# A gated attention and quantised layer on one core: the first key tile or the values move ahead of the output projection, and the opening is rewritten

## The reference

```python
x = x + tanh(g_xattn) * attention(layernorm(x), ctx, Wq, bq, Wk, bk, Wv, bv, Wo, bo)   # 16 heads of 32
x = x + tanh(g_ffn) * quantised(layernorm(x), weight_q, weight_scale, bias)

def quantised(x, weight_q, weight_scale, bias):
    x_scale = max(amax(|x|), 1e-6) / 127
    x_q = clip(round(x / x_scale), -128, 127)
    return (x_q @ weight_q.T) * x_scale * weight_scale + bias
```

## Time and profile before

| what | us |
|---|---|
| median of 3 runs | 916.76 |
| lowest and highest of these | 912.73, 916.80 |
| the profiled execution | 920.62 |
| its span, first to last instruction | 918.8 |
| PE busy | 836.2 (91% of the span) |
| DVE, ACT, POOL busy | 538.7, 513.4, 525.7 (56 to 59%) |
| first instruction of step 0 on PE | 76.07 after the span's start |

### The profile page before, as it was taken

The page is one execution under the profiler, slowest core; times in us unless marked ns, Lnnn a source line. Parts: engine busy times, 40 slices in busy tenths (PEclk is TensorE's granted clock), DMA queues, the critical chain, the costliest instruction groups (busy, mean ns, idle before and its releaser), DMA issues.

```text
span 918.8 us, 16063 instructions
## 1 busy us (share of the span) xinstructions
PE 836.2 (91%) x6304; PEld 522.9 (57%) x6304; DVE 538.7 (59%) x746; ACT 513.4 (56%) x708; POOL 525.7 (57%) x552
## 2 busy tenths in 40 slices
PE   4549989999999999999999999999999999999784
PEld 3336546656565666656565666656565666655451
DVE  2754365656655676656655676656655675654444
ACT  2323445656566665656566665656566665655633
POOL 0541344747475765747475755747475755745565
PEclk9777889999999999999999999999999999999997
DMA  8145031322314142312314142422314131111101
GB/s 269 43 143 164 26 120 46 119 69 64 122 41 144 47 147 65 126 61 68 121 47 138 47 145 68 119 74 60 122 42 144 35 116 46 35 49 44 59 24 68
DMA packets 39755, 80.15 MB, mean 87 GB/s; under 512 B 7168, under 2 KB 7808, under 8 KB 37632
## 3 DMA queue, kind: packets, MB, share of 16 engines
q1 hardware_dynamic: 38560, 77.97, 26.8%
q10 hardware_dynamic: 1120, 1.16, 0.4%
HBM read 62.30 MB, written 16.81 MB: 86 GB/s over the span
## 4 chain that ended last, share of the span: by engine, by line
PE 60%; DVE 13%; POOL 13%; issue 7%; DMA 3%; ACT 3%; SPq 0%; ACTq 0%; POOLq 0%; DVEq 0%
PE bank_a L298 22%; PE scores L331 6%; PE pv_ps L360 5%; PE bank_b L298 5%; PE scores L346 5%; PE sum_ps L362 5%; POOL x L1040 5%; DVE row_max L817 4%; PE bank_b L384 3%; POOL x L1053 3%; POOL o_lo L1044 3%; DVE q_unit L852 2%; PE bank_b L315 2%; DVE u_sb L862 1%; DVE q_amax L846 1%
## 5 line engine op out<-in xcount | busy, mean ns | idle before, releaser
L817 DVE TENSOR_REDUCE row_max<-scores 128x16 f32<-128x1920 f32 x64 | 138.2, 2159 | 158.5 <-PE scores L331 158.4
L1053 POOL TENSOR_TENSOR x<-x,u_sb 128x512 f32<-128x512 f32 x64 | 85.7, 1340 | 152.7 <-DVE u_sb L862 150.4
L604 ACT ACTIVATE probs<-scores 120x2048 f32<-120x2048 f32 x64 | 120.4, 1882 | 68.9 <-PE scores L350 68.9
L1044 POOL TENSOR_TENSOR o_lo<-on,o_hi 128x512 fp32r<-128x512 f32 x64 | 88.0, 1374 | 113.9 <-ACT o_hi L620 113.9
L807 DVE TENSOR_TENSOR xt_lo<-xt,xt_hi 128x512 fp32r<-128x512 f32 x64 | 69.6, 1108 | 96.6 <-ACT xt_hi L571 96.2
L1048 POOL TENSOR_TENSOR x<-x,gbias_r 128x512 f32<-128x512 f32 x64 | 82.3, 1287 | 51.9 <-ACT cen L626 51.6
L298 PE MATMUL bank_a<-xt_hi,wq_hi 128*128 128x512 f32 x248 | 106.1, 428 | 4.8 <-ACT v_sb L590 4.8
L1015 POOL TENSOR_TENSOR xt<-xt,rstd_b 128x512 f32<-128x512 f32 x64 | 100.2, 1591 | 16.6 <-DMA rstd_b<-rstd_rows 11.8
L331 PEld LDWEIGHTS scores<-k_sb,q_sb 32*128 32x128 f32 x2048 | 63.7, 188 | 64.7 <-issue 51.4
L298 PE MATMUL bank_a<-xt_lo,wq_hi 128*128 128x512 f32 x248 | 99.0, 399 | 0.0
L298 PE MATMUL bank_a<-xt_hi,wq_lo 128*128 128x512 f32 x248 | 98.9, 399 | 0.0
(11 more groups left out here) (155 smaller groups left out, 1663.4 us busy)
## 6 DMA issues: line engine op xcount, KB each, us to landing
xt<-in_x_t SPq DMA_DIRECT2D x16, 1024.0 KB, 5.5
x<-in_x SPq DMA_DIRECT2D x64, 256.0 KB, 3.0
out_x<-x SPq DMA_DIRECT2D x64, 256.0 KB, 2.1
x_in<-in_x SPq DMA_DIRECT2D x62, 256.0 KB, 3.8
rstd_b<-rstd_rows SPq DMA_DIRECT2D x16, 256.0 KB, 5.0
ctx_sb<-in_ctx_t SPq DMA_DIRECT2D x7, 360.0 KB, 5.0
probs<-in_wq SPq DMA_DIRECT2D x1, 1024.0 KB, 9.9
x<-in_wo SPq DMA_DIRECT2D x1, 1024.0 KB, 13.3
```

Source lines behind the costliest of these rows:

```text
L604: act.activation(probs[0:KEYS], scores[0:KEYS], ACT.Exp, scale=SCALE).then_inc(p_ready, 1)
L817: dve.tensor_reduce(row_max[:].rearrange("p (t r) j -> p r t j", r=ROWG)[:, :, :, j], scores[:, :, 0:QT * KEYS].rearrange("p r (t k) -> p ...
L1044: pool.tensor_tensor(o_lo[i % 2][:, j], on[:, j % 2], o_hi[i % 2][:, j].bitcast(F32), ALU.subtract).then_inc(o_split, 1)
L1053: pool.tensor_tensor(x1_of(m)[:, t], x1_of(m)[:, t], u_sb[:], ALU.add).then_inc(out_ready, 1)
```

## The change

**In every step.** In part 0 `project_k(pair, 0)` or `project_v(n - 1)` now comes right behind `scores_by_query(b, 0)`, in `bank_b`, and `project_o(m, 0)` behind it, in `bank_a`. `project_k(pair, 1)` follows in `bank_b` and waits for `k_ready` of the first key tile. In part 2 the same is done with `project_k(pair, 2)` or `project_v(n)` in `bank_a`, ahead of `project_o(m, 2)` in `bank_b`. ACT's `bias_k` or `copy_v` moves ahead of `high_o`. The banks of the neighbouring projections are exchanged to fit.

**In the front.** The inverse deviations of batches 0 and 1 no longer go through DRAM: PE spreads them over the partitions by four transposes into `sum_ps` (`spread_rstd`). For batch 0 DVE multiplies xt by it (`scale_x0`); for batch 1 ACT copies it to `rstd_b` and POOL multiplies as before. DVE alternates scaling xt, centring Wq and the rest of xt; POOL takes the rest of Wq. Wv is staged in `x1[1]` and loaded early, the tiles of batch 1 use `cen` as well, xt of batch 1 is loaded ahead of the five small constants. The splitting of Wo, the bias row (`fold_bias`, `fold_rows`) and the cast of the integer weights move into step 0, and POOL's four `bias_x` of batch 0 to the end of that step. The first `project_k` no longer waits for the bias of the keys.

```diff
             def load_x(n, t):
-                sp.wait_ge(x_stats, nth(n, QT, t) - 2 if n > 1 or t >= 2 else nth(0, QT, t))
-                load(x_landed[t % 2], x_in[:, t % 2], x_v[n, t])
+                if n == 1 and t >= 2:
+                    load(x1st_landed[t - 2], cen[:, t - 2, 0:D], x_v[n, t])
+                else:
+                    sp.wait_ge(x_stats, nth(0, QT, t) if n == 1 else nth(n, QT, t) - 2)
+                    load(x_landed[t % 2], x_in[:, t % 2], x_v[n, t])
...
+            def spread_rstd(n):
+                pe.wait_ge(x_pool, nth(n, 2, 1))
+                if n > 0:
+                    pe.wait_ge(x_scaled, nth(n - 1, DT, 3))
+                for t in range(QT):
+                    ins = pe.transpose(sum_ps[:, t * P:(t + 1) * P], ln_rstd[:, t:t + 1].broadcast_to([P, P]), ident_f[:])
+                ins.then_inc(rstd_spread, 1)
...
                 if is_batch(b):
                     scores_by_query(b, 0)
+                if i == 0:
+                    pe.wait_ge(v_ready, nth(1, 1))
+                if keys_next:
+                    project_k(pair, 0, bank_b)
+                if values_next:
+                    project_v(n - 1, bank_b)
                 if is_batch(m):
                     pe.wait_ge(o_split, nth(m, DT, 3))
-                    project_o(m, 0, bank_b)
+                    project_o(m, 0, bank_a)
                 if keys_next:
-                    project_k(pair, 0, bank_a)
-                    if is_batch(m):
-                        pe.wait_ge(x1_ready, nth(m, QT, 0))
+                    pe.wait_ge(k_ready, nth(pair, DT, 0))
                     project_k(pair, 1, bank_b)
-                if values_next:
-                    project_v(n - 1, bank_a)
...
+                if i == 0:
+                    fold_bias(bank_a)
...
-            project_q(0, 2, pv_ps)
+            project_q(0, 2, bank_a)
+            spread_rstd(1)
             pe.wait_ge(max_done, nth(0, DT, 0))
             scores_by_query(0, 1)
-            project_q(0, 3, bank_a)
+            project_q(0, 3, bank_b)
...
                 log_sums(i, 0)
                 invert_sums(i, 0)
+                if i == 0:
+                    act.wait_ge(wo_gated, 1)
+                    act.activation(flat(wo_hi), flat(wo_stage), ACT.Copy).then_inc(wo_hi_done, 1)
...
+                if keys_next:
+                    bias_k(pair, 0, bank_b)
+                if values_next:
+                    copy_v(n - 1, bank_b)
                 high_o(i, 0)
...
+            def scale_x0(c):
+                dve.wait_ge(rstd_spread, 1)
+                dve.wait_ge(xt_landed, 16)
+                dve.tensor_tensor(xt[:, c], xt[:, c], sum_ps[:], ALU.mult).then_inc(x_scaled, 1)
```

More of the change, by code:

```diff
@@ L237, in _ @@
             load(rest_landed, ident_b[:], consts_bf16)
-            load_xt(1)
-            for t in range(QT):
-                load_x(2, t)
+            load_x(2, 0)
+            load_x(2, 1)
             load_ctx(1)
+            load_x(2, 2)
+            load_x(2, 3)
             load_x(3, 0)
@@ L385, in quantised_layer, with fold_bias @@
                 ins.then_inc(ffn_done, 1)
+            def spread_rstd(n):
+                pe.wait_ge(x_pool, nth(n, 2, 1))
+                if n > 0:
+                    pe.wait_ge(x_scaled, nth(n - 1, DT, 3))
+                for t in range(QT):
+                    ins = pe.transpose(sum_ps[:, t * P:(t + 1) * P], ln_rstd[:, t:t + 1].broadcast_to([P, P]), ident_f[:])
+                ins.then_inc(rstd_spread, 1)
+            def fold_bias(bank):
+                pe.wait_ge(wo_gated, 1)
+                pe.wait_ge(bv_landed, 16)
+                for c in range(DT):
+                    ins = pe.matmul(bank[:], bv_c[:, c:c + 1].broadcast_to([P, P]), wo_stage[:, c],
+                                    start=c == 0, stop=c == DT - 1)
+                ins.then_inc(bv_ready, 1)
             def step(i):
@@ L501, in _ @@
             pe.wait_ge(consts_ready, 5)
-            pe.wait_ge(bk_landed, 16)
             pe.wait_ge(wk_landed, 16)
-            for j in range(DT):
-                project_k(0, j, scores[:, j])
+            project_k(0, 0, scores[:, 0])
+            project_k(0, 1, scores[:, 1])
+            pe.wait_ge(ident_landed, 16)
+            spread_rstd(0)
             pe.wait_ge(wq_landed, 16)
@@ L756, in _ @@
                 act.activation(wv_hi[:, c], wv_stage[:, c], ACT.Copy).then_inc(wv_hi_done, 1)
-            bias_q(0, 3, bank_a)
-            for c in range(DT):
-                high_x(1, c)
-            copy_v(0, bank_b)
+            bias_q(0, 1, bank_b)
+            bias_q(0, 2, bank_a)
+            act.wait_ge(rstd_spread, 2)
+            act.activation(rstd_b[:].rearrange("q (p t) -> q t p", t=QT), sum_ps[:].rearrange("q (t p) -> q t p", t=QT),
+                           ACT.Copy).then_inc(rstd_copied, 1)
+            bias_q(0, 3, bank_b)
+            high_x(1, 0)
+            copy_v(0, bank_a)
+            high_x(1, 1)
+            high_x(1, 2)
+            high_x(1, 3)
+            copy_v(1, bank_b)
             high_max(0)
-            copy_v(1, sum_ps)
-            copy_max(0, bank_a)
-            act.wait_ge(wv_lo_done, CT)
+            copy_max(0, pv_ps)
             for i in range(0, B):
@@ L942, in _ @@
             low_ctx(0)
-            dve.wait_ge(wq_mean, 1)
-            for c in range(DT):
-                dve.tensor_tensor(wq_stage[:, c], wq_stage[:, c], pv_ps[:], ALU.subtract).then_inc(wq_centred, 1)
-            for c in range(DT):
-                dve.wait_ge(wq_hi_done, c + 1)
-                dve.tensor_tensor(wq_lo[:, c], wq_stage[:, c], wq_hi[:, c].bitcast(F32), ALU.subtract).then_inc(wq_lo_done, 1)
+            scale_x0(0)
+            centre_wq(0)
+            scale_x0(1)
+            low_x(0, 0)
+            centre_wq(1)
+            scale_x0(2)
+            low_x(0, 1)
+            centre_wq(2)
+            scale_x0(3)
+            low_x(0, 2)
+            centre_wq(3)
+            low_x(0, 3)
+            for t in range(QT):
+                x_statistics(1, t)
+            maxima(0, 0)
+            x_statistics(2, 0)
+            x_statistics(2, 1)
+            maxima(0, 1)
+            low_x(1, 0)
+            low_x(1, 1)
+            maxima(0, 2)
+            low_x(1, 2)
+            low_x(1, 3)
+            maxima(0, 3)
+            low_max(0)
             dve.wait_ge(gates_ready, 1)
@@ L1094, in step @@
                 low_o(i, 3)
+                if i == 0:
+                    pool.wait_ge(bias_folded, 1)
+                    bias_x(i, 0)
+                    bias_x(i, 1)
                 bias_x(i, 2)
```

230 lines of the change are left out of this document (115 added, 115 removed).

## The result

| what | before | after |
|---|---|---|
| median of 4 runs each, us | 915.47 | 884.57 |
| lowest and highest | 912.73, 916.80 | 884.04, 886.75 |
| the profiled execution | 920.62 | 884.38 |
| its span | 918.8 | 882.6 |
| first instruction of step 0 on PE | 76.07 | 56.31 |

The ratio is 0.9671, with a 95% interval of 0.964 to 0.9701. The forecast was 883.2 us.

A forecast was written before the change was run, and what follows sets the result against it. PE bounds the loop; the front waits for data, DVE's gated Wo and a maximum. 920.62 - 19.6 (front) - 1.7 (step 0) - 12.3 (loop) = 887.0; the gain of 33.6 from 916.76 gives 883.2 us, range 876 to 896.5.

The forecast's parts named there:

- Step 0 starts at 56.5, gain 19.6: Front: step 0 begins at 56.5 us instead of 76.07, gain 19.6, bounds 53 and 61.
- First queries at 26.5, DVE the pace: Front: DVE's scalings, centrings and splits set the pace; PE ends the first query projection at 26.5 us, not 40.
- Clock in the front: Front: granted clock falls once near 23 us, PE idle between keys and queries, and once behind the 4.1 wait.
- Step 0, -1.7: Step 0: added bias product, key-bias waits and clock effects sum to -1.7 us, bounds -4 and +3.
- The -2.9: Step 0: the fold fills the 2.28 us wait, so the half-clock stretch from 97 to 103 may go, -2.9 us.
- Loop, 12.3: Loop: PE's waits go, 7.5 us in six steps with keys, 4.8 in six with values; bounds 9 to 13.
- From the trace to the median: Whole run: 887.0 us for the profiled execution; the same gain of 33.6 from 916.76 gives 883.2.
- A: Rival: front at half clock throughout, from short waits; +10 us, 893; chance 0.13.
- B: Rival: a new wait, project_k(1) behind quant_round at the quantiser's old pace, eats the loop's gain; +12.3, 895.5; chance 0.10.
- C: Rival: DVE's scalings and splits in the front collide with POOL, 1.7 us each; +7.5, 890.7; chance 0.06.
- D: Rival: ACT's early key bias holds o_hi, o_lo and normalise_o, slowing the loop; 3.0 us a step, 922; chance 0.02.
- E: Rival: front's tiles of batch 2 land late, at 40 us, behind xt and constants; +4, 887; chance 0.06.

The follow-up runs named there:

- max_first: Changed kernel with DVE's third and fourth maxima in the front moved ahead of splits of batch 1; 878.98 us, ratio 0.9604.
- after_again: The changed kernel, unchanged, run again for a second trace; 884.75 us, ratio 0.9681.
- the two repeats: Second traces of the unchanged kernels, before_again and after_again; 916.85 us in one run and 884.75 us.
- loop_only: Kernel before with the change's order of PE's projections, banks and ACT's reads in every step, old front kept; 905.81 us, ratio 0.9888.
- copy_first: Kernel before with only ACT's copy_v(n - 1) moved ahead of high_o in steps with values; 911.69 us, ratio 0.9952.
- act_late: Changed kernel with ACT's part 0 bias_k and copy_v back behind high_o and integers, PE's new order kept; 927.07 us in one run.
- before_again: The kernel before, unchanged, run again for a second trace; 916.85 us in its one run.
- fold_late: Changed kernel with fold_bias and fold_rows moved from part 1 of step 0 to part 3; 882.7 us, ratio 0.9643.
- tuned_late: Changed kernel with max_first's order, high_max(0) ahead of copy_v(1), wo_hi behind step 0's part 1 exponentials, fold in part 3; 877.29 us, ratio 0.9578.

## Why the prediction was right

- **Step 0 starts at 56.5, gain 19.6.** Measured 56.31 and 19.8. The wait of 4.1 behind `high_x` and `low_x` was 4.00, and `max_first` shows its cause, since it vanishes with DVE's order. The fourth query projection ended at 40.15, said was 40.
- **First queries at 26.5, DVE the pace.** Right to 1.1 us (27.62), for a partly wrong reason. Three splits were to pay 1.1 more each beside POOL; only the last paid 0.5. The price fell on POOL, which was not in the sum (1.6 for 1.27), and PE waited 2.5 us for POOL's `wq_lo`. The scalings were sized right, 0.68 for 0.65. Keys 0 and 1 took 4.65, not 3.3, and keys 2 and 3 later 2.59: the first of these matmuls last up to 0.74 us and the later ones 0.37, though the granted clock reads 1.00 for both, so half of the old 6.56 was not the price of the first half.
- **Clock in the front.** One fall near 23 and one behind the long wait were let in. These stretches of the changed kernel show both (columns as in the earlier trace rows). The first is not certain: it is in the traces of after, `after_again` and `max_first`, and in none of the other five with the new front.

```profile
24.00:28.00 4.00, 3.61 (x8) 2.47 (x9) 3.76 (x9) 0.54 (x2) 1.68 (x3) 0.50 0.55 178
48.00:52.00 4.00, 4.00 (x38) 3.24 (x35) 2.83 (x3) 0.00 (x0) 0.00 (x0) 0.50 0.01 4
```

- **Step 0, -1.7.** Measured -1.37 between the first two traces and +0.19 between the two repeats. The parts are there (1.3 for the fold's place for 1.1, 1.0 ahead of the second key tile for 1.3, 0.6 in part 2 for 0.5), but the two large terms are the clock's. The start at full clock, -1.7, is there in the first trace and not in `after_again`, where the granted clock is 0.51 and 0.64 from 56 to 60 us. The -2.9, for a fall behind the 2.28, need not be the fold's: `loop_only` keeps that wait and had no fall behind it. The total hangs on the clock, so the traces bear it out only within its bounds of -4 and +3. The prediction did not see the 3.43 at the end of the step, the better place for added work.
- **Loop, 12.3.** Measured 13.6: 8.0 in the steps with keys (1.28 in each of five, 1.62 in one) for 7.5, and 5.5 in those with values for 4.8. The extra 0.1 in a step with values is not explained; `copy_first` alone gave 0.85, also more than the wait of 0.81. Step 1 is 0.6 shorter between the first two traces and 0.2 longer between the repeats, so nothing can be read from it.
- **From the trace to the median.** The traces differ by 36.2 and the medians by 30.9. The parts of the first are 19.76 + 1.37 + 0.57 + 13.55 + 0.91 at the end, 36.2 in all. The profiled execution of before lay 5.2 above its median, that of after at its median. The prediction took 3.9 of this off by carrying the gain over to the median; that the gain itself, read from a high execution, could hold some of the excess, it did not consider. The gain between the traces is 5.3 above that between the medians, and the sum was 2.6 below the gain between the traces (1.3 in the loop, 0.9 at the end, 0.6 in step 1, 0.2 in the front, less 0.3 in step 0). The two cancelled in part, and 33.6 was forecast for 30.9. That the forecast lies only 1.4 from the measured 884.57 is partly luck: it was taken from 916.76, 1.3 above the 915.47 of the four runs.
- **Rivals.** A: no, the clock is 0.50 in two stretches, not from 25 to 50. B: no, the steps follow PE's new pace. C: only in POOL's share above. D: no; `act_late`, which puts ACT's bias the other way round, costs 2.7 us in the mean of the twelve steps against the changed kernel, as much as D needed, but by PE's wait and the clock and not by D's chain (fourteen steps, 0 to 13, make keys or values, not D's thirteen). E: not in the two traces of the changed kernel, where DVE waited 0.2 us at most for the tiles. But `act_late`, with the same front, has it with a wait of PE of 2.1 us, so it comes in some executions of this front, below the 4 that it was priced at.

## What to carry to other kernels

When two producers share a pair of banks, ask of each reader what stands ahead of it in its own engine's order: moving one copy on ACT took out a wait that looked like a matter of PE, and the same move of PE's work without it was slower than no change (927 us in one run, for 916). A wait of 2 to 3 us on a dense PE should be priced twice, once as itself and once with the half clock behind it, since here both happened (53.8 and 55.4 to 56.9 us for the same kind of step in `act_late`). Before filling a gap with moved work, list all gaps: here a larger one stood 20 us further on.

## What the runs showed of the hardware that was not expected

- The same code with the same wait meets a falling clock in one trace and not in the next. A wait of 2.28 us in step 0 was followed by stretches at 0.50 in the kernel before, in `before_again` and in `copy_first`, and by none in `loop_only`, `fold_late` and `tuned_late`. The wait of 3.43 us at the end of step 0 was followed by one in all ten traces that have it. Of six waits of about 2.8 us inside a dense loop in `act_late` four were. The price of a fall was 1.6 to 3.1 us in these steps.
- A POOL difference of 1.27 us took 1.52 to 1.61 with a DVE split beside it. Where the split began first it kept its 0.68, and where POOL was already running it took 1.18 and 1.06. In these rows the one that comes second pays.
